# Half-width value units, a third row buffer, matmuls that keep TensorE occupied, and one block in place of two, in an audio layer with experts

## The reference, cut to what matters

```
h = lin(0.5 * (ewma forward + ewma backward)(W_ve diff(x) + b_ve))   # 16 x 750 x 128
q, k, v = LN(h) wq', wk', wv' (+ biases), 8 heads of 16
h = h + silu(LN(h) wg' + bg) * ((q k' / 4) * decay, causal) v        # retention, no softmax
r = LN(h), logits = r Wr (8 experts), probs = softmax over all 12000 tokens
for each expert: its 1024 tokens of highest prob (top_k)
h = h + prob * (gelu(r W1 + b1) W2 + b2), added at those tokens
```

## Time and profile before

| | us |
|---|---|
| median of three runs | 631.08 (630.94 to 636.57) |
| the profiled execution's own time | 635.75 |
| its span, first to last instruction | 634.0 |

### The profile page before, as it was taken

How to read it: one execution, slowest core, us unless ns; L and a number is a source line. 1 busy time by engine, 2 the same in 40 slices (tenths; PEclk the granted TensorE clock), 3 DMA queues, 4 the chain that set the end, 5 groups by cost and what they waited for, 6 DMA issues and landing times. The chain is left out here.

```text
span 634.0 us, 15489 instructions
## 1 busy us (share of the span) xinstructions
PE 488.3 (77%) x6262; PEld 350.0 (55%) x6262; DVE 406.6 (64%) x797; ACT 288.4 (45%) x545; POOL 355.2 (56%) x267
## 2 busy tenths in 40 slices
PE   4799989999899999999724543258779797797880
PEld 3457656776477777777514442235555565556650
DVE  5444895768766677777647777875766767765110
ACT  1455643556435666666204442036444563445640
POOL 7047743577335865555400000176787878888874
PEclk9889997999889999999955555559797897987996
DMA  6210132132222323321241000012442534424232
GB/s 242 56 33 4 44 83 66 37 84 58 67 77 56 84 51 79 79 78 54 56 122 38 0 0 1 7 35 57 64 78 50 70 63 62 76 48 72 49 30 25
DMA packets 45139, 37.01 MB, mean 58 GB/s; under 512 B 5842, under 2 KB 39186, under 8 KB 44948
## 3 DMA queue, kind: packets, MB, share of 16 engines
q1 hardware_dynamic: 33176, 25.85, 15.1%
q0 software_dynamic: 11264, 8.72, 10.2%
q10 hardware_dynamic: 636, 1.54, 0.7%
HBM read 12.89 MB, written 16.96 MB: 47 GB/s over the span
## 5 line engine op out<-in xcount | busy, mean ns | idle before, releaser
L752 POOL TENSOR_TENSOR prob<-prob,cst 125x1000 f32<-125x1000 f32 x48 | 102.6, 2138 | 87.6 <-ACT prob L639 87.6
L1393 POOL DMA_INDIRECT out<-y,idx_add x64 | 101.8, 1590 | 18.3 <-issue 16.9
L639 ACT COPY prob<-ps_score 125x1000 f32<-125x1000 f32 x48 | 47.6, 992 | 90.5 <-PE ps_score L418 90.4
L1371 POOL DMA_INDIRECT taken<-rows_dram,idx x64 | 69.8, 1091 | 19.3 <-issue 18.7
L1543 DVE TENSOR_TENSOR slot_hot<-numbers,bank 125x4096 bf16<-125x4096 bf16 x18 | 79.4, 4412 | 0.0
L1250 PE MATMUL bank<-takenT,w_sb 128*128 128x512 f32 x128 | 71.7, 700 | 1.7 <-ACT hidden L1325 1.1
L1259 PEld LDWEIGHTS bank<-w_sb,hidden 128*128 128x128 f32 x512 | 58.4, 192 | 24.1 <-ACT hidden L1325 24.1
L1259 PE MATMUL bank<-w_sb,hidden 128*128 128x128 f32 x512 | 61.3, 278 | 11.7 <-ACT hidden L1325 11.7
L1325 ACT ACTIVATE hidden<-bank,b_sb 128x512 f32<-128x512 f32 x64 | 43.6, 687 | 51.7 <-PE bank L1250 51.6
L886 DVE TENSOR_TENSOR prob<-ps_score,cst 125x1000 f32<-125x1000 f32 x48 | 57.4, 1196 | 9.1 <-PE ps_score L418 9.0
L1360 POOL TENSOR_TENSOR carrier<-cst 1x1 f32<-1x1 f32 x25 | 10.1, 403 | 94.6 <-DVE idx L1556 88.7
(11 more groups left out here) (184 smaller groups left out, 919.7 us busy)
## 6 DMA issues: line engine op xcount, KB each, us to landing
rows_dram<-row_sb SPq DMA_DIRECT2D x16, 404.3 KB
out<-row_sb SPq DMA_DIRECT2D x16, 375.0 KB
w_sb<-in_L_ffn_W SPq DMA_DIRECT2D x16, 256.0 KB
r_in<-smooth SPq DMA_DIRECT2D x32, 93.8 KB, 3.7
e_in<-s_norm SPq DMA_DIRECT2D x32, 93.8 KB, 2.1
cst<-in_consts SPq DMA_DIRECT2D x1, 1703.0 KB
xin<-in_x ACTq DMA_DIRECT2D x4, 375.0 KB, 7.3
taken<-rows_dram,idx POOLq DMA_INDIRECT x64, 2.6
```

Of the source, the lines that this page charges most:

```text
L639: act.copy(prob[no % 2][:, 2:4, :, :].rearrange("p g c i -> p g (c i)"), ps_score[0:C, 2:4, 0:4 * C]).then_inc(high_copied, 1)
L752: pool.tensor_tensor(scores, scores, const("mask", C)[:, H // 2 * C:].rearrange("p (g i) -> p g i", g=2) .unsqueeze(2).broadcast_to([C, 2, ...
L1371: pool.indirect_dma_start(out=taken[it.slot][:, g, :], out_offset=None, in_=rows_dram[:, :], in_offset=bass.IndirectOffsetOnAxis(ap=idx[it ...
L1393: pool.indirect_dma_start(out=out_rows[:, :], out_offset=bass.IndirectOffsetOnAxis(ap=idx_add[it.slot][:, g:g + 1], axis=0), in_=y[it.slot ...
```

## The change

It has four parts. **(1) Value units:** `value_units` and `w_v` go; `token_units` is used for the values too (six matmuls of 128 columns, two units), and ACT's two copies (the later chunks first) place each head's 16 columns between zeros that DVE writes once at the start. An item has 16 units in the ring. **(2) Rows and smoothing:** three row buffers in place of two; in the two steps with a smoothing, `smooth_sum` and the row statistics move from the end of the step into the next, behind its first masked scores. **(3) `keep_warm`:** matmuls without a reader, of 512 or 128 columns, stand before PE's waits in the search and up to the first expert, and seven more end PE's list of stage 1. **(4) One block:** the second block goes; PE and SP wait for the sixteenth kept logits instead, and the other engines come after PE by their own waits.

```diff
-VALUE_CHUNKS = ((4, 5), (2, 3), (1,), (0,))
+ROW_BUFS = 3
+SPLIT = 2 * D + 2 * DH
...
-            order += [(u, n + 1) for u in ("t0", "t1", "v0", "v1", "v2", "v3")]
+            order += [(u, n + 1) for u in ("t0", "t1", "v0", "v1")]
...
-        block = nc.Block()
-        stage1.enter_context(block)
+        block = ctx.enter_context(nc.Block())
...
             def state_unit(it):
                 pe.wait_ge(read["t1"], it + 1)
-                pe.wait_ge(read["v2"], it + 1)
+                pe.wait_ge(read["v0"], it + 1)
...
                 if after is not None:
-                    token_units(after)
+                    token_units(after, "t", 1)
                     scores(after, 0)
-                    value_units(after, (0, 1))
-                    value_units(after, (2, 3))
+                    token_units(after, "v", 2)
...
             all_steps(step)
+            pe.wait_ge(high_copied, B * PAIRS)
+            for k in range(7):
+                pe.matmul(ps_score[:, 3, :], const("centre"), const("projections"), start=True, stop=True)
...
             def rows(it, k):
-                if k == 0 and it >= 2:
-                    act.wait_ge(logits_kept, it - 1)
-                    act.wait_ge(h2_out[it % 2], it // 2 * 16)
-                    act.wait_ge(rows_out[it % 2], it // 2 * 16)
+                if k == 0 and it >= ROW_BUFS:
+                    act.wait_ge(logits_kept, it - ROW_BUFS + 1)
+                    act.wait_ge(h2_out[it % ROW_BUFS], it // ROW_BUFS * 16)
+                    act.wait_ge(rows_out[it % ROW_BUFS], it // ROW_BUFS * 16)
...
             def values_out(it, k):
-                if k == 0 and it >= 2:
+                if k == 1 and it >= 2:
                     act.wait_ge(valued, (it - 1) * PAIRS)
                 act.wait_ge(filled[f"v{k}"], it + 1)
-                first, n = VALUE_CHUNKS[k][0], len(VALUE_CHUNKS[k])
-                act.copy(v_split[it % 2][:, first:first + n, :].rearrange("p c d -> p (c d)"),
-                         bank_of(f"v{k}", it)[0:C, 0:n * 2 * D]).then_inc(read[f"v{k}"], 1)
+                own_half = v_split[it % 2][:, k * HALF:(k + 1) * HALF, :].rearrange("p c (e y) -> p c e y", e=2)
+                act.copy(own_half[:, :, :, 0:D].rearrange("p c e (g z) -> p c e g z", z=2 * DH)[:, :, :, :, 0:DH],
+                         bank_of(f"v{k}", it)[0:C, 0:HALF * D].rearrange("p (c g e d) -> p c e g d", c=HALF, e=2, d=DH)
+                         ).then_inc(read[f"v{k}"], 1)
...
             dve.memset(diff[:, 0:1], 0.0).then_inc(diff_done, 1)
+            for k in range(2):
+                dve.memset(v_split[k][:, :, :], 0.0).then_inc(zeros_set, 1)
...
                     low_scores(own, 1)
+                if n - 1 in SMOOTH_AT:
+                    smooth_sum(SMOOTH_AT[n - 1])
+                    norm_stats(last, 0)
+                    norm_stats(last, 1)
                 if last is not None:
                     norm_moments(last)
...
-                if before is not None:
+                if before is not None and not j:
                     norm_stats(before, 0)
                     norm_stats(before, 1)
                 if own is not None:
                     gated_out(own, 2)
-                if j:
-                    smooth_sum(j)
...
-        block = ctx.enter_context(nc.Block())
...
+            sp.wait_ge(logits_kept, B)
             load(item(0))
...
+            def keep_warm(n, to, width=512):
+                for k in range(n):
+                    pe.matmul(to[:, 0:width], const("centre"), const("projections")[:, 0:width], start=True, stop=True)
+
+            pe.wait_ge(logits_kept, B)
             for c in range(NC):
...
+            keep_warm(2, banks[7])
             pe.wait_ge(dve_step, 2)
...
+            keep_warm(1, banks[7])
             with pe.Fori(0, ROUNDS // UNROLL) as i:
                 for j in range(UNROLL):
...
                     pe.wait_ge(thresholds_set, r + 1)
                     pe.matmul(banks[5][:, 0:3], const("same_expert"), const("sign_base"), start=True, stop=False,
                               skip_group_check=True)
+                    keep_warm(5, banks[7], 128)
                     pe.wait_ge(counted_act, r + 1)
...
                               skip_group_check=True).then_inc(totals_done, 1)
+                    keep_warm(2, banks[7], 128)
+
+            keep_warm(6, banks[7])
             pe.wait_ge(rows_ranked, 1)
...
+            keep_warm(3, banks[3])
             pe.wait_ge(place_done, 1)
...
+            keep_warm(5, banks[3])
+
             def index(it):
...
+                        if early(it, 1) and t:
+                            keep_warm(1, banks[3])
...
             index(item(0))
+            keep_warm(4, banks[3])
             pe.wait_ge(exp_sums_done, 1)
...
+            keep_warm(8, banks[3])
             pe.wait_ge(inverse_done, 1)
```

More of the change, by code:

```diff
@@ L196, in program @@
         logits = sb("logits", [C, NC, B * E])
-        row_sb = [sb(f"row_sb{k}", [C, NC, ROW]) for k in range(2)]
+        row_sb = [sb(f"row_sb{k}", [C, NC, ROW]) for k in range(ROW_BUFS)]
         stage1 = ExitStack()
@@ L238, in program @@
         k_tok = s1("k_tok", [C, NC, D])
-        v_split = [s1(f"v_split{k}", [C, NC, 2 * D]) for k in range(2)]
+        v_split = [s1(f"v_split{k}", [C, NC, SPLIT]) for k in range(2)]
         gate = [s1(f"gate{k}", [D, T]) for k in range(2)]
@@ L353, in step @@
                 if last is not None:
[L354 removed]
+                    slot = last % ROW_BUFS
                     sp.wait_ge(row_done, last + 1)
@@ L503, in gate_units, with token_units @@
                               start=True, stop=True).then_inc(filled[f"g{k}"], 1)
-            def token_units(it):
-                ps = [claim(f"t{k}", it) for k in range(2)]
+            def token_units(it, name, w):
+                ps = [claim(f"{name}{k}", it) for k in range(2)]
                 for c in range(HALF):
@@ L510, in token_units @@
                                       e_in[it % PER_BLOCK][at:at + CH + 2, chunk(k * HALF + c)],
-                                      w_raw[at:at + CH + 2, 1, :], start=True, stop=True)
+                                      w_raw[at:at + CH + 2, w, :], start=True, stop=True)
                         if c == HALF - 1:
[L513 to L522, removed]
-                        m = pe.matmul(o[0:C, i * 2 * D:(i + 1) * 2 * D],
-                                      e_in[it % PER_BLOCK][at:at + CH + 2, chunk(VALUE_CHUNKS[k][i])],
-                                      w_v[at:at + CH + 2, :, :].rearrange("p w d -> p (w d)"), start=True, stop=True)
-                        if i == last:
-                            m.then_inc(filled[f"v{k}"], 1)
+                            m.then_inc(filled[f"{name}{k}"], 1)
             def state_unit(it):
                 pe.wait_ge(read["t1"], it + 1)
-                pe.wait_ge(read["v2"], it + 1)
+                pe.wait_ge(read["v0"], it + 1)
                 ps = claim("s", it)
@@ L720, in step @@
                     high_scores(after, 0)
-                    for k in range(4):
+                    for k in (1, 0):
                         values_out(after, k)
```

50 lines of the change are left out of this document (19 added, 31 removed).

## The result

The changed kernel takes 607.23 us (median of three, 605.21 to 610.17) where the kernel before takes 631.08: a ratio of 0.96, 95 % interval 0.950 to 0.970. I had forecast 590 and a range of 582 to 605: the sign was right, the gain of 23.9 is little more than half of the 41.1 forecast. The profiled execution took 610.17 with a span of 608.4, so 25.6 less than before by spans.

| span, us | before | changed | gain | forecast | gain with the repairs (589.68 us, below) |
|---|---|---|---|---|---|
| start to the first state matmuls | 38.8 | 37.7 | 1.1 | 0 | 0.9 |
| sixteen items (A and B) | 273.5 | 256.5 | 17.0 | 27.5 | 30.6 |
| passage, to the turned logits (C) | 12.6 | 5.9 | 6.7 | 6.1 | 6.7 |
| search to the first list (D) | 82.4 | 81.3 | 1.0 | 7.5 | 8.5 |
| experts | 226.8 | 227.1 | -0.3 | 0 | 0.0 |

What follows compares the result with a forecast made beforehand. PE's list was taken to bound undisturbed stage 1 items, with waits bounding smoothings, passage and search rounds. Gains 12.9 + 14.6 + 6.1 + 7.5 = 41.1 us off the 631.08 median made 590, range 582 to 605.

Steps and rivals of the forecast that it cites:

- A: Stage 1 items, new value units: 0.94 us saved in each of fifteen steps, less 1.2 for steps 6 and 10: 12.9 us.
- B: Items after the smoothings of steps 2 and 6: sum and statistics moved, 7.3 us saved each, 14.6 in all.
- C: Passage from stage 1 to the search: third row buffer and no second block, seven fills end last; 6.1 us saved.
- D: Search: small matmuls in series run faster if the clock is 2.4 GHz, 5.6 us of it in the rounds; 7.5 saved.
- DVE's narrow margin: Stage 1 item: DVE's statistics end at 252.09, its gating is due at 252.25, a margin of 0.16 us.
- the list of what could be late next: Stage 1 with shorter PE work: ACT's two copies (0.49 us each) and DVE's gating checked; nothing lost at that value.
- the sign of about 18: Items after steps 2 and 6: about 18 us at a clock of 1.00 would show the smoothing's forecast gain.
- products at 88.5, PE needs them only for its last projection: Item after step 2: products 3.1 us behind the state matmuls, wanted about 2.7 us in; excess left 1.0.
- the sign of half a smoothing: Items after steps 2 and 6: a sum of 2.70 us would point to 4 gained instead of 7.3 each; 597, chance 0.08.
- no wait of PE in the search is over about 1 us, so I take 2.4 GHz: Search: with fillers PE's waits are short enough to keep the clock at 2.4 GHz, on which 7.5 us depend.
- the first rival: Search: clock stays at 1.2 GHz and fillers lie on PE's path, 1.4 us more a round; 640 us, chance 0.05.
- The third rival: Stage 1: another engine takes over, items shrink by 0.15 to 0.6 us rather than 0.94; 595 to 602, chance 0.20.

Runs made afterwards that it cites:

- the repairs: Changed kernel plus POOL's second-pair mask waiting for the state's scan, 3, 1 (256 columns) and 2 fills before the rounds, next item's first mask held until its scan: 589.68 us.
- the hold: Changed kernel with one more wait on POOL: the mask of an item's second score pair waits until DVE's state scan has ended; 597.27 us, ratio 0.940.
- the copy freed: Changed kernel with second-pair mask waiting for the state's scan, more fills before the rounds, and next item's first mask waiting for DVE's spreading copy: 595.23 us.

## Why the prediction was too low

**Value units: the size right, the neighbours missed.** An undisturbed item lost 1.00 (forecast 0.94), the period is 14.70 (14.8), ACT's copies take 0.49 as assumed, and DVE's narrow margin held. The memsets, 1.50 each, put the first subtraction off by 0.08. The step that failed is the list of what could be late next: ACT's copies and DVE's gating stood on it, DVE's copy at 0.6 in steps 6 and 10, and the state's scan not at all. By the forecast's own terms steps 6 and 10 and the items after steps 2 and 6 were to take 16.8, 16.2, 17.3 and 17.3; they took 18.62, 18.62, 22.97 and 18.43. That is 11.1 us, and the items as a whole fell short by 10.5. I had seen that DVE's instructions stretch under POOL's mask, and applied it to copy and sum alone. The state's scan reads two operands in SBUF too; the kernel before never shows it under a mask (0.49 in all sixteen items). But the price of such a scan was in that trace. The backward scan of the smoothing, the same operation, takes 1.75 us there at the start and 3.73 beside a mask:

```profile
L823 DVE TENSOR_TENSOR_SCAN bwd<-keep,last_diff,diff x4: 1752/2854/3727, 7.8 to 160.0; 128x750 f32<-128x750 f32 x4
...
84.28 2.14 POOL L752 TENSOR_TENSOR prob<-prob,cst 125x1000 f32<-125x1000 f32 x1 [1.60 <-ACT prob L639]
```

The Trainium skill has the rule ("SBUF — State Buffer", section "Who interferes with whom"): a DVE instruction with two SBUF inputs contends with a GpSimd instruction that reads SBUF. The traces here agree: for the state's scan 0.49 alone, 2.07 and 2.29 beside the mask. In the changed kernel and in all experiments the backward scans of steps 2 and 6 still stand under that mask (3.72 in step 2 of the changed kernel), just ahead of the gating and the products; what freeing them would give, no run here shows.

**Smoothing: right by itself, half lost beside the value units.** With the old units the two items after a smoothing fall from 25.53 and 25.52 to 17.19 and 17.18, 8.3 each (forecast 7.3, upper bound 8.3). With the new units and the hold it is 17.24, or 1.0 above item and norm units, the excess forecast (17.3 by the sum; the sign of about 18 that I gave was too wide to tell it from the 18.43 with a collision). As changed they were 22.97 and 18.43. The step that failed is "products at 88.5, PE needs them only for its last projection": the products did come 2.85 after the state matmuls, as the forecast's 3.1 has it, but what PE needs behind them is the scan, and POOL's mask started 0.40 before it. I summed the two parts as if each kept the other's timing; A also counts 0.94 for each of these two items, which take 17.2 with old and new units alike. The sum of 0.92 there, where 2.70 was to be the sign of half a smoothing, told nothing: PE waited for another instruction, and where the item took 17.24 and 17.19 the sum met a mask and took 2.08 and 2.04, at no cost.

**The passage: right.** 6.7 us against 6.1; the fills end last, 5.85 after the last output matmuls (6.5).

**The search: the clock, for five rounds.** At 2.4 GHz a round is 2.91 (forecast 2.95), and the kernel with the clock held gains 8.5 of 82.4 (7.5). One small matmul takes 0.36 to 0.38 there and not the 0.30 that I read from a row of two, so each gains 0.21 and not 0.29; but the round gains both in full, 0.41. The step that failed is "no wait of PE in the search is over about 1 us, so I take 2.4 GHz": the waits of 0.86, 0.57 and 0.40 are all under that, and the clock fell behind them. Then the first rival's mechanism ran for five rounds: 4.35 at 0.50 with the fills on PE's path (4.7 forecast). It ended where the clock rose, which that rival did not have. Against the 7.5 forecast the changed kernel gained 1.0: its rounds cost 0.9 more than before in place of 5.6 less. The section of the Trainium skill that I set against the forecast ("TensorE: Matmul & The Clock Gate", "A second HAM failure mode: psum-queue depth-cycling") tells of a kernel whose clock goes up and down with short idle times between groups of matmuls. In the rounds nothing of the kind shows here: five kernels run all 16 at 1.00 in such groups. Ahead of the rounds the fall behind the waits of 0.86 and 0.57 is like it.

**The chances.** The third rival, another engine in stage 1 (0.20, 595 to 602), was nearest in kind: DVE took over, in the steps with extra work on DVE and POOL rather than in every item. None of the cases had losses in stage 1 and in the search together; 10.5 and 6.5 make 17 us, which the range did not hold. That the best kernel's 589.68 is nearly the 590 forecast is luck: its items gained 30.6 where 27.5 were forecast, with a copy kept off the mask, which the forecast did not have, and it ran on another chip.

## What to carry to other kernels

When a part of the change makes one engine's list shorter, list every instruction of another engine that shares a resource with a third, and write down how far it now starts from the one that it collides with: 0.4 us decided here over 1.6 us of stall and, in three of its four places, a fall of the clock behind it. Two gains that lie in the same step are not to be added before the second has been placed on the timeline that the first makes. Fills that hold a clock have to cover the way to a loop as well as the loop, and each is to be priced at the low clock too, where it stands on the path.

## What the runs showed of the hardware

- In the collisions of DVE with POOL's mask shown here DVE's instruction ended a little less than its own time after the mask: in the changed kernel the state's scan 0.34 us after it (0.49 alone), the copy 0.41 (0.55 alone), the backward scan 1.58 (1.75 alone). Sparing one instruction can hand the wait to the next: with the copy freed (2.43 to 0.55), the scan behind it took 2.29.
- A clock that has fallen can stay low under a busy engine: PE was busy 17.54 of 17.56 us at 0.50 in the first rounds of the search before it rose. Why it rose in the fifth round and not sooner, no run here tells.
- How long the clock stays low moves an item's time with no change to its instructions: the item after step 2 took 22.97, 19.82, 19.97 and 19.92 in four kernels with the same stage 1.
